# Two stored copies of the scan's rows, and reads of 16 distinct rows, in a four-layer kernel on one Trainium2 core

## The reference

```
delta = softplus(u @ w_xproj[:, :8] @ w_dt + b_dt)      # the time step, one value for each t and d
Bm, Cm = the other columns of u @ w_xproj               # 16 states each, for each t
dA = exp(delta[d] * A[d, n])
h  = dA * h + (delta * u)[d] * Bm[n]                    # for t = 0 .. 255
y[d] = sum over n of h[d, n] * Cm[n]
```

## Time and profile before

| | us |
|---|---|
| Median of 3 runs | 2742.13 |
| Lowest and highest of the 3 | 2737.71, 2745.82 |
| The profiled execution | 2738.4 |
| Span in its profile | 2737.1 |

### The profile page before, as it was taken

How to read it: one execution, slowest core, us unless ns; L and a number is a source line. 1 busy time by engine, 2 the same in 40 slices (tenths; PEclk the granted TensorE clock), 3 DMA queues, 4 the chain that set the end, 5 groups by cost and what they waited for, 6 DMA issues and landing times.

```text
span 2737.1 us, 46943 instructions
## 1 busy us (share of the span) xinstructions
PE 2218.0 (81%) x17922; PEld 1564.0 (57%) x18077; DVE 1987.8 (73%) x4099; ACT 1401.9 (51%) x3576; POOL 819.3 (30%) x460
## 2 busy tenths in 40 slices
PE   4777887777774779999999999778898876888886
PEld 2445554555442646666666666546565555666665
DVE  3389899989888527777777777656666625888887
ACT  1355555555554127777776767424343333545453
POOL 0034334343345102323332323200000002555553
PEclk9899999998987869999999999989999997989988
DMA  2077787777789920000000000000100003445553
GB/s 79 18 183 190 174 197 176 182 183 181 178 196 227 291 86 1 1 1 1 1 1 2 1 1 1 22 13 23 31 21 8 6 26 124 143 169 164 172 175 115
DMA packets 108863, 257.78 MB, mean 94 GB/s; under 512 B 11744, under 2 KB 49888, under 8 KB 108128
## 3 DMA queue, kind: packets, MB, share of 16 engines
q1 hardware_dynamic: 106592, 250.58, 33.8%
q0 software_dynamic: 2048, 4.20, 0.5%
HBM read 236.40 MB, written 17.81 MB: 93 GB/s over the span
## 4 chain that ended last, share of the span: by engine, by line
PE 49%; DVE 22%; ACT 12%; issue 8%; DMA 7%; SPq 1%; POOL 0%; another core or an unknown queue 0%; POOLq 0%; DVEq 0%; ACTq 0%
DMA h<-dtu_rows 6%; PE psum L324 3%; PE psum L683 3%; DVE h L1487 3%; PE psum L679 3%; PE psum L490 3%; ACT pr L1831 3%; PE psum L731 3%; PE psum L570 3%; ACT dA L1783 2%; PE psum L615 2%; PE psum L401 2%; PE psum L690 2%; PE psum L428 2%; ACT pt L1875 2%
## 5 line engine op out<-in xcount | busy, mean ns | idle before, releaser
L2074 POOL TENSOR_TENSOR h<-h,Crep 128x1024 f32<-128x1024 f32 x128 | 322.4, 2520 | 566.7 <-DVE h L1487 566.7
L2058 POOL TENSOR_TENSOR pr<-pr,rsum 128x512 f32<-128x512 f32 x192 | 236.0, 1236 | 547.0 <-DVE rsum L1368 547.0
L1487 DVE TENSOR_TENSOR_SCAN h<-dA,h 128x1024 f32<-128x1024 f32 x128 | 305.0, 2385 | 16.8 <-ACT dA L1971 16.7
L1402 DVE TENSOR_REDUCE mx<-psum 128x4 f32<-128x1024 f32 (+1 forms) x192 | 230.2, 1216 | 106.5 <-PE psum L688 106.5
L1875 ACT ACTIVATE pt<-psum 128x1024 f32<-128x1024 f32 x192 | 189.0, 1020 | 143.8 <-PE psum L690 143.7
L1971 ACT ACTIVATE dA<-dA,A 128x255 f32<-128x255 f32 x512 | 215.7, 499 | 74.9 <-DMA dA<-delta_rows 74.5
L2108 POOL TENSOR_TENSOR h<-h,Crep 128x1024 f32<-128x1024 f32 x64 | 179.7, 2809 | 220.0 <-DVE h L1293 219.7
L1831 ACT ACTIVATE pr<-psum,nb 128x256 f32<-128x256 f32 (+1 forms) x512 | 210.5, 429 | 15.5 <-DVE nb L1360 14.5
L1841 ACT ACTIVATE prT<-psum 128x512 f32<-128x512 f32 x192 | 116.1, 604 | 148.7 <-PE psum L584 146.7
L1480 DVE TENSOR_TENSOR h<-h,psum 128x1024 f32<-128x1024 f32 x128 | 153.1, 1208 | 43.0 <-DMA h<-dtu_rows 42.8
L490 PE MATMUL psum<-h,pack_wf 128*128 128x256 f32 x512 | 162.8, 474 | 15.9 <-POOL h L2108 15.9
(11 more groups left out here) (331 smaller groups left out, 5028.5 us busy)
## 6 DMA issues: line engine op xcount, KB each, us to landing
dA<-delta_rows SPq DMA_DIRECT2D x128, 512.0 KB, 8.1
h<-dtu_rows SPq DMA_DIRECT2D x128, 512.0 KB, 8.7
Brep<-bc_rows SPq DMA_DIRECT2D x64, 512.0 KB, 4.1
Crep<-bc_rows SPq DMA_DIRECT2D x64, 512.0 KB, 5.5
w1r<-m_w SPq DMA_DIRECT2D x32, 256.0 KB, 6.4
w2r<-m_w SPq DMA_DIRECT2D x32, 256.0 KB
dtu_rows<-dtu SPq DMA_DIRECT2D x64, 64.0 KB, 1.7
delta_rows<-delta SPq DMA_DIRECT2D x64, 63.8 KB, 2.0
```

The lines of the kernel that those rows point to most:

```text
L1402: ve.e.tensor_reduce(mx[:, qb, 2 * h:2 * h + 2, groups[0]:groups[-1] + 1], k.psum[:, base:base + 2, :].rearrange("p i (n x) -> p i n x", n ...
L1487: ve.e.tensor_tensor_scan(flat(h), flat(k.dA[n % NDA]), flat(h), 0.0, ALU.mult, ALU.add).then_inc(*k.set("scanned", 0, n))
L2058: po.e.tensor_tensor(p3, p3, bcast(k.rsum[n][:, 0:len(heads[r])], P * (q + 1), 2), ALU.mult).then_inc(*k.set("normed", 1, b, p, r))
L2074: po.e.tensor_tensor(h[:, :, :], h[:, :, :], bcast(k.Crep[b % 2][:, :], 4, 1), ALU.mult).then_inc(*k.set("hC", 0, n))
```

## The change

The two scratch tensors hold each row twice, in two copies `u` that lie next to each other: [2, 2, 32, 2 (u), 4, 256]. Every store is issued twice, once for each copy, and so is the zeroing store of the load phase. A read of a group now takes the 16 rows (8 channels x 2 copies) as its outermost entries, and repeats each 8 times, so that partition p holds channel p // 16 and state p % 16. The constants that depend on this order (`pick`, the columns of `w_brep` and `w_crep`, `A_log0`) are permuted on the host; their shapes stay.

```diff
 def stored_rows(k, l, b, name, rows, src, first):
     sp = k.sp
     for s in range(4):
-        sp.e.dma_start(rows[b % 2, :, :, s, first:].rearrange("c m t -> m c t"), src[32 * s:32 * s + 32, :, first:]).then_inc(
-            *k.set(f"{name}_stored{b % 2}", l, b, by=16))
+        for u in range(2):
+            sp.e.dma_start(rows[b % 2, :, :, u, s, first:].rearrange("c m t -> m c t"), src[32 * s:32 * s + 32, :, first:]).then_inc(
+                *k.set(f"{name}_stored{b % 2}", l, b, by=16))

 def read_rows(k, rows, b, c, j):
-    return bcast(rows[b % 2, c, 8 * j:8 * j + 8, :, :].rearrange("m s t -> m (s t)"), NS, 0)
+    return bcast(rows[b % 2, c, 8 * j:8 * j + 8, :, :, :].rearrange("m u s t -> (m u) (s t)"), NS // 2, 1)
...
-    sp.e.dma_start(k.delta_rows.rearrange("i c (m r) s t -> (i c m) (r s t)", r=1), flat(k.h[0])).then_inc(*k.set("delta_stored0", "zero", by=16))
+    for u in range(2):
+        sp.e.dma_start(k.delta_rows[:, :, :, u].rearrange("i c m s t -> (i c m) (s t)"), flat(k.h[0])).then_inc(*k.set("delta_stored0", "zero", by=16))
...
-    k.delta_rows, k.dtu_rows = (nc.dram_tensor(x, [2, CI, 32, 4, L], F32, kind="Internal").ap() for x in ("delta_rows", "dtu_rows"))
+    k.delta_rows, k.dtu_rows = (nc.dram_tensor(x, [2, CI, 32, 2, 4, L], F32, kind="Internal").ap() for x in ("delta_rows", "dtu_rows"))
...
-    rows = np.arange(P)[:, None, None] % 8
+    rows = np.arange(P)[:, None, None] // NS
...
-    put("w_brep", np.repeat(xp[:, :, DTR:DTR + NS], 8, 2))
-    put("w_crep", np.repeat(xp[:, :, DTR + NS:], 8, 2))
+    put("w_brep", np.tile(xp[:, :, DTR:DTR + NS], (1, 1, 8)))
+    put("w_crep", np.tile(xp[:, :, DTR + NS:], (1, 1, 8)))
...
-    put("A_log0", g["L0_attn_A_log"].reshape(CI, 4, 4, 8, NS).transpose(4, 3, 0, 2, 1).reshape(P, 8, 4))
+    put("A_log0", g["L0_attn_A_log"].reshape(CI, 4, 4, 8, NS).transpose(3, 4, 0, 2, 1).reshape(P, 8, 4))
```

## The result

The changed kernel takes 2793.74 us (median; 2793.21 to 2807.77), the kernel before 2740.35 in the same comparison. The ratio is 1.0211, with a 95% interval of 1.0187 to 1.0234: slower by 2.1%. The forecast of a slower kernel held, and so did the place where the time is lost, but the cost was set too low. On the median before of the prediction, 2742.13, the ratio gives 2800 us, 22 above the forecast of 2778 and 2 above the range's upper end of 2798.

A forecast was written before the change was run, and what follows sets the result against it. VectorE was taken to bound layer 0's scan, busy 89%. Later reads 46 us, minus 10 of mid-turn waits, plus 0.4 load phase gave +36 us: 2774 on the profiled execution, 2778 us against the median; range 2735 to 2798.

The forecast's parts named there:

- the bound and the place: Layer 0's scan: VectorE bounds, busy 89%; later reads lengthen its wait for h(1) near each turn's (batch's) end.
- The argument from layer 3: Layer 3 reads one shared row at 416 GB/s, so the copy's split slows layer 0's reads; they stay at 237.
- the price of the stores: SyncE's four more delta and four more dtu issues delay the four reads: 46 us, 2.9 a turn.
- a turn of the second kind: Seven of 16 batches: four delta issues take 1.73 us, SyncE then waits 1.04 for dtu; dA(0) 2.43 us later.
- the first kind of turn: Nine of 16 batches: four delta issues take 2.56 us, dtu's begin 0.22 us after; dA(0) 3.25 us later.
- The upper bound of 4.3 a turn: SyncE's extra delta issues as slow as the held-up ones, 2.56 + 1.74 us a batch, 69 us in all.
- the likeliest case's own range: Whole kernel's time if it slows as forecast, with the lower and upper costs of the stores: 2757 to 2801 us.
- what VectorE gives back: Layer 0, mid-turn: with VectorE 2.9 us later, reads come before it needs them; 10 us of waits for `h` go.
- Faster reads: Layer 0's reads: the crowded source was the cost, distinct rows reach 416 GB/s; about -27 us, 2715; chance 0.20.
- No change: Layer 0: VectorE's 88.6 idle us shrink elsewhere as much as they grow; 2742 to 2752, say 2746 us; chance 0.10.
- Slower by more through bytes that collide: Doubled stores collide with reads: 4.3 us a turn, about 2800 us; counted inside the forecast's chance of 0.70.
- The lock-stepped streams: Streams aliasing in HBM, by which distinct rows would help layer 0's reads; the 416 GB/s from one shared row disagrees.

The follow-up runs named there:

- the run with the reads alone: Against the kernel before: reads of the change, each store issued once, second copy left at the load phase's zeros; 2744.82 us, ratio 1.0019.

## Where the prediction was right, and the terms that it sized wrongly

**Right: the bound and the place.** VectorE's busy time did not move, and the loss is its wait for h(0) and h(1) at the turn's end, with h(0) newly among them. The reads stayed at 240 GB/s, h(1) came 11 us after dA(0)'s issue, and the load phase lost 0.43 us (VectorE's first step at 22.76 instead of 22.33), for 0.4 forecast. The turn became 51.7 us long (774.9 us from the first turn's delta store to the sixteenth's, before 723.9, over 15), where "about 50.5" was expected. The argument from layer 3, that what makes these reads slow is the split of the copy and not the shared source, was borne out: distinct rows in the old split stayed at 242 GB/s, and one shared row in the other split ran at 321 over a burst.

**Wrong: the price of the stores.** This is the step that failed. The term "30 + 16 = 46 us, 2.9 a turn" measured 63 us, 3.95 a turn, and VectorE felt 56 of them. Two parts of it were off. The chain of waits in a turn of the second kind shows the 16 issues one by one (start, us):

```profile
551.22 0.31 SPq L2176
551.57 0.43 SPq L2176
...
557.33 2.18 SPq L2176
559.56 0.43 SPq L2176
```

First, I took the span of the first four issues, 1.73 us, for the price of four more. Only the first issue of a row is short, 0.31 us; the rest are 0.43 to 0.45 us and 0.04 apart. Four more cost 1.94 (eight took 3.67 where nothing held them), and dtu's eight took 3.80, 2.06 more. Together that is 0.53 us a turn, some 8 us in all. Second, one issue in that turn took 2.18 us. Before, such a held-up issue lay among delta's in the first kind of turn, and I counted the second kind as free of it. Now five of the seven turns of the second kind have it among dtu's, where nothing hides it: 8.5 to 9.4 us from the first delta store to dA(0) instead of 4.6, nearly twice the lateness that I had worked out (2.43). The two turns without it have 7.6, so in the five it makes another 8 us. The upper bound of 4.3 a turn did hold the 3.95, and the likeliest case's own range, up to 2801, the 2800; the range that I gave stopped at 2798.

**Wrong, smaller: what VectorE gives back.** "Those 10 us of waits go" came to less than 3: the mid-turn waits are 7.7 us after, 10.3 before. Added up by the measured terms: 56 more at the turns' ends, 2.7 less in mid-turn, 4 more for `dA` (20.5 against 16.7, put at nothing in the sum), and 0.4 in the load phase are 57 to 58, against 55.3 in the span.

**The rivals.** Faster reads: out, by the burst at 240 GB/s and the run with the reads alone. No change: out, since the other waits of VectorE hardly shrank (those for TensorE by 3 us, those for `zab` by 3). Slower by more through bytes that collide: the same bytes behind the reads cost 0.35%, and in two issues 0.73% with dA(0) 0.9 us later a turn, so the bytes are at most a small part. The lock-stepped streams that the prediction took from the Trainium skill, "DMA: Bandwidth & Descriptors", section "Latency and other measured facts", are told there of rows 512 KiB and more apart. The rows here lie 4 KB apart, so the runs neither bear that out nor refute it.

## What to carry to other kernels

Count the DMA issues that stand in a queue ahead of the transfer for which the bound engine waits: here each cost 0.42 to 0.49 us, from 16 to 256 KB, and moving them behind that transfer left a sixth of the loss. Price one more issue from the middle of a row of issues, not from the first few, and ask whether the longer row takes in an issue that is held up. And before changing what a slow transfer reads, compare it with a fast one in the same trace: here the way in which the copy was split decided, and the number of distinct rows mattered far less.

## What the runs showed of the hardware that I had not expected

One store issue in many turns is held up, to 1.74 us at 288.23 and 2.18 at 557.33 in the changed kernel. In the second case the transfers took 23% of the DMA engines' time, so a lack of room there does not explain it. The DMA view of 557 to 559.6 has one packet on the instruction queue:

```profile
q1 hardware_dynamic: 206, 0.16, 22.6%
q8 instruction: 1, 0.02, 4.1%
```

The same view of 550 to 554, when nothing was held up, has none. Asked for all store issues above 0.7 us, the view shows such a packet of 16 KB beside 14 of the 15 in the changed kernel and beside all 8 in the kernel before. In the seven turns of the second kind it shows none among the stores before; with the row of stores twice as long, five of them have one. That is the part of the lateness that I had not counted. The packets do not look like SyncE's own instructions: the change adds 129 instructions, all on SyncE, and the page counts 143 packets on that queue in both kernels, one for every 252 of TensorE's 35,999 matmuls and weight loads. Why an issue of SyncE stands still beside such a packet no run tested.

A store of 16 pieces took SyncE as long to issue as one of 64 (0.42 us each, in the kernel that has both). Where nothing held it up, a read of 128 partitions took 0.51 to 0.60 us with 16 outermost and as long with 32, and 0.32 to 0.44 with 128 outermost.
